# Turning ten of a kernel's sixteen feed-forward chunks by VectorE and a DRAM trip instead of by TensorE, on one core

## The reference

```
x = x + 0.5 * ffn(LN(x))      # FFN1
x = x + attention(LN(x))      # 16 heads of 8 features
x = x + 0.5 * ffn(LN(x))      # FFN2

ffn(x):  h = x @ W1' ; h = gelu(h + b1)          # 512 hidden features
         y = h @ W2' + b2
         W1' = W1.T + scale * (products of two normalized tokens of this batch)
         W2' the same for W2, from other tokens of the first 16
attention(x): q', k' = exp(q R/sqrt8 - |q|^2/16), the same for k
         kv = k'.T @ v  per batch and head;  out = q' @ kv / (sum q' + 1e-8) @ Wo.T + bo
```

## Time and profile before

| | before |
|---|---|
| median of three runs | 175.92 us (175.82 to 176.13) |
| time of the profiled execution | 174.35 us |
| its span (first to last instruction) | 172.6 us |
| TensorE busy | 166.8 us (97%), 1132 matmuls |
| VectorE busy | 127.4 us (74%) |
| ScalarE busy | 123.2 us (71%) |
| GpSimd busy | 69.4 us (40%) |
| bytes moved | 9.06 MB |

### The profile page before, as it was taken

How to read it: one execution, slowest core, us unless ns; L and a number is a source line. 1 busy time by engine, 2 the same in 40 slices (tenths; PEclk the granted TensorE clock), 3 DMA queues, 4 the chain that set the end, 5 groups by cost and what they waited for, 6 DMA issues and landing times.

```text
span 172.6 us, 3454 instructions
## 1 busy us (share of the span) xinstructions
PE 166.8 (97%) x1132; PEld 148.8 (86%) x1132; DVE 127.4 (74%) x446; ACT 123.2 (71%) x241; POOL 69.4 (40%) x85
## 2 busy tenths in 40 slices
PE   6999999999999999999999999899999999999993
PEld 6976998898899989768788898789899989898893
DVE  1888798977967647899999999998957664651111
ACT  3498669598796958779955499986894757557500
POOL 4522196232188089862522544004451399200000
PEclk9999999999999999999999999999999999999999
DMA  4993100404000000000000004310005003521203
GB/s 107 291 281 100 50 0 3 124 4 122 2 0 4 0 2 4 0 0 0 0 0 6 0 4 122 91 36 2 4 8 176 0 0 88 161 90 32 66 13 108
DMA packets 17009, 9.06 MB, mean 53 GB/s; under 512 B 1008, under 2 KB 16608, under 8 KB 16992
## 3 DMA queue, kind: packets, MB, share of 16 engines
q1 hardware_dynamic: 16704, 8.85, 17.4%
q10 hardware_dynamic: 288, 0.00, 0.1%
HBM read 6.69 MB, written 2.15 MB: 51 GB/s over the span
## 4 chain that ended last, share of the span: by engine, by line
PE 90%; DVE 5%; issue 2%; ACT 1%; POOL 0%; POOLq 0%; DVEq 0%; ACTq 0%
PE quad L728 32%; PE quad L712 9%; PE quad L713 9%; PE quad L714 9%; PE ps_t L677 4%; PE quad L745 4%; PE quad L663 4%; PE quad L747 3%; PE quad L746 3%; PE ps_g L763 3%; PE ps_m L700 2%; PE ps_t L785 2%; PE ps_r L752 1%; DVE s L604 1%; PE ps_g L728 1%
## 5 line engine op out<-in xcount | busy, mean ns | idle before, releaser
L728 PEld LDWEIGHTS quad<-w2e,gl 128*128 128x128 f32 x496 | 59.9, 192 | 2.4 <-ACT gl L432 0.2
L728 PE MATMUL quad<-w2e,gl 128*128 128x128 f32 x496 | 60.7, 275 | 0.0
L432 ACT ACTIVATE gl<-quad,cols 128x512 f32<-128x512 f32 x64 | 43.5, 686 | 20.6 <-PE quad L714 20.3
L712 PE MATMUL quad<-xh,w1h 128*128 128x512 f32 x64 | 28.7, 448 | 0.6 <-DVE w1l L568 0.2
L342 POOL TENSOR_TENSOR rstd<-veps,mhalf 128x4 f32<-128x4 f32 (+1 forms) x16 | 16.1, 1011 | 31.3 <-DVE veps L124 29.5
L399 ACT ACTIVATE xn<-X,nmr,rstd 128x128 f32<-128x128 f32 x61 | 24.8, 484 | 3.6 <-DVE nmr L499 3.6
L713 PE MATMUL quad<-xl,w1h 128*128 128x512 f32 x64 | 25.3, 395 | 0.0
L714 PE MATMUL quad<-xh,w1l 128*128 128x512 f32 x64 | 25.2, 394 | 0.0
L595 DVE TENSOR_TENSOR X<-quad,X 128x512 f32<-128x512 f32 (+1 forms) x16 | 10.8, 673 | 15.6 <-PE quad L728 9.9
L363 POOL TENSOR_TENSOR X<-X,b2h 128x512 f32<-128x512 f32 x16 | 20.6, 1311 | 4.1 <-issue 4.1
L374 POOL TENSOR_TENSOR qn<-qk,zr 128x512 f32<-128x512 f32 x8 | 8.6, 1081 | 23.7 <-DVE zr L625 23.6
(11 more groups left out here) (108 smaller groups left out, 279.7 us busy)
## 6 DMA issues: line engine op xcount, KB each, us to landing
ev<-token_rows SPq DMA_DIRECT2D x7, 512.0 KB, 3.7
X<-in_x_dram SPq DMA_DIRECT2D x7, 256.0 KB, 6.4
out_dram<-X SPq DMA_DIRECT2D x7, 256.0 KB, 2.9
w1t<-in_w1t_dram SPq DMA_DIRECT2D x1, 256.0 KB, 3.6
w2n<-in_w2t_dram SPq DMA_DIRECT2D x1, 256.0 KB, 4.7
wa<-in_wa_dram SPq DMA_DIRECT2D x1, 256.0 KB, 6.7
out_dram<-X SPq DMA_DIRECT2D x2, 128.0 KB, 1.8
X<-in_x_dram SPq DMA_DIRECT2D x1, 192.0 KB, 3.3
```

Of the source, the lines that this page charges most:

```text
L432: act.activation(gl[:, f % 2, j], ps_h[j % 2], ACT.Gelu, bias=cols[:, j:j + 1]).then_inc(s_gelu, 1)
L712: pe.matmul(ps_h[j % 2], w1h[:, w, blk], xh[:, f % XT], start=True, stop=False)
L728: ins = pe.matmul(y[:, n * P:(n + 1) * P], gl[:, f % 2, j, n * P:(n + 1) * P], w2e[:, f // PER_B % 2, j], start=(j == 0), stop=(j == HB - 1))
```

## The change

- Chunks 4 to 7 and 10 to 15 no longer use TensorE's transposes. The new VectorE stage **blocks** transposes the 32x32 blocks of xn into the tile tq (a ring of two). SyncE's **put** writes tq to DRAM (256 KB), and **land** reads it back in four transfers of 64 KB whose pattern puts the blocks in their places, into the tile land (a ring of three). ScalarE's and VectorE's halves of **turn** then read land in SBUF instead of ps_t in PSUM. Chunks 0 to 3, 8 and 9 go on as before.
- Attention's inputs are still turned by TensorE, but xah and xal become rings of six chunks.
- **z_eps** goes from VectorE to GpSimd; the second half of **mix** (the copy of mo) goes from VectorE to ScalarE; batch 0's rounding of W1' (**first_w1h**) goes from VectorE to ScalarE.
- The first loads are issued in another order: X of chunk 3 ahead of W2, X of chunk 4 ahead of the bias rows, and the attention weights last. W2 is scaled in place.
- All five lists of ORDER are rewritten; **constants** now comes ahead of batch 1's weights.

The core of the diff (the rewritten lists are cut down to a few of their places):

```diff
+PE_TURNS = (0, 1, 2, 3, 8, 9)
+BY_DRAM = [f for f in range(FC) if f not in PE_TURNS]
+SQ = 32
+LAND, TQ, AH = 3, 2, 6
...
 "sp":
+        "rows.1 rows.2 put.4 land.4 put.5 rows.3 put.6 land.5 land.6 put.7 land.7 rows.4 rows.5 put.10 land.10 put.11 "
...
 "act":
+        "norm.0 rest.0 first_w1h.0 first_w1h.1 turn.0 norm.1 first_w1h.2 norm.2 turn.1 up.0.0 first_w1h.3 up.0.1 "
+        "load.0 up.0.2 up.0.3 turn.2 up.1.0 up.1.1 norm.3 up.1.2 norm.4 up.1.3 w1h.1 norm.5 turn.3 up.2.0 up.2.1 "
...
 "dve":
+        "scale.0 stats.0 moments.0 rest.0 norm.0 stats.1 rest_norm.0 odd.0 moments.1 first_w1.0 first_w1.1 stats.2 "
+        "norm.1 moments.2 first_w1.2 first_w1.3 stats.3 norm.2 turn.0 first_w1l.0 first_w1l.1 moments.3 first_w1l.2 "
+        "stats.4 stats.5 first_w1l.3 turn.1 moments.4 w2.0 norm.3 norm.4 stats.6 stats.7 moments.5 moments.6 turn.2 "
+        "odd.1 norm.5 w1.1 constants.0 b2h.0 w1l.1 blocks.4 blocks.5 w2.1 norm.6 turn.3 down.0.3 moments.7 astats.0 "
...
 "pe":
+        "warm_up.0.0 warm_up.0.1 lead.0 select.0 turn.0 select.1 warm_up.0.2 turn.1 up.0.0 up.0.1 up.0.2 up.0.3 "
+        "turn.2 up.1.0 up.1.1 down.0.0 up.1.2 up.1.3 down.0.1 turn.3 down.0.2 down.0.3 down.1.0 down.1.1 up.2.0 "
...
+        def turned(f):
+            return as_tiles(ps_t[:]) if f in PE_TURNS else in_order(land[:, by_dram(f) % LAND])
...
+                if stage == "put":
+                    sp.wait_ge(s_tr, by_dram(i) + 1)
+                    sp.dma_start(folded[i], tq[:, by_dram(i) % TQ]).then_inc(s_put[i], 16)
+                if stage == "land":
+                    sp.wait_ge(s_put[i], 16)
...
+                    for b in range(D // SQ):
+                        place = slice(SQ * b, SQ * (b + 1))
+                        sp.dma_start(land[place, by_dram(i) % LAND].rearrange("p (q c) -> p q c", q=P // SQ),
+                                     folded[i].rearrange("(q p) (b c) -> b p q c", p=SQ, c=P)[b]).then_inc(s_land[i], 16)
...
                 if stage == "turn":
-                    act.wait_ge(s_xt, i + 1)
+                    if i in PE_TURNS:
+                        act.wait_ge(s_xt, by_pe(i + 1))
+                    else:
+                        act.wait_ge(s_land[i], 16 * D // SQ)
                     wait(act, s_u, HB * (i - XT + 1))
-                    act.activation(xh[:, i % XT], ps_t[:], ACT.Copy).then_inc(s_hi, 1)
+                    act.activation(as_tiles(xh[:, i % XT]), turned(i), ACT.Copy).then_inc(s_hi, 1)
...
+                if stage == "blocks":
+                    dve.wait_ge(s_xn, normed(i, NT - 1))
+                    k = by_dram(i)
+                    if k >= TQ:
+                        dve.wait_ge(s_put[BY_DRAM[k - TQ]], 16)
+                    dve.transpose(folding(tq[:, k % TQ]), as_tiles(flat(xn[:, i % XN]))).then_inc(s_tr, 1)
```

More of the change, by code:

```diff
@@ L34 @@
     "sp": (
-        "rows.1 rows.2 rows.3 rows.4 rows.5 rows.6 down.8.3 rows.7 down.9.3 down.10.3 down.11.3 down.12.3 down.13.3 "
-        "down.14.3 down.15.3 "
+        "rows.1 rows.2 put.4 land.4 put.5 rows.3 put.6 land.5 land.6 put.7 land.7 rows.4 rows.5 put.10 land.10 put.11 "
+        "rows.6 put.12 land.11 land.12 put.13 rows.7 put.14 land.13 land.14 down.8.3 put.15 land.15 down.9.3 "
+        "down.10.3 down.11.3 down.12.3 down.13.3 down.14.3 down.15.3 "
     ),
     "pool": (
[5 rows of a table removed]
[5 rows of a table added]
     ),
     "act": (
[13 rows of a table removed]
[13 rows of a table added]
     ),
     "dve": (
[17 rows of a table removed]
[18 rows of a table added]
     ),
     "pe": (
[17 rows of a table removed]
[17 rows of a table added]
     ),
@@ L150, in build @@
         xl = sb("xl", [P, XT, TOK], F32R)
+        tq = sb("tq", [P, TQ, TOK])
+        land = sb("land", [P, LAND, TOK])
         abst = sb("abst", [P, CHUNKS, NT, 6])
@@ L233, in build @@
             sem(n) for n in ("r_bst", "r_mv", "r_veps", "r_rstd", "r_nmr", "r_xn", "s_lead")]
+        s_tr = sem("s_tr")
+        s_put = [sem(f"s_put{f}") for f in range(FC)]
+        s_land = [sem(f"s_land{f}") for f in range(FC)]
         s_u, s_gelu, s_d = sem("s_u"), sem("s_gelu"), sem("s_d")
@@ L261, in xslot, with by_dram, by_pe, folding @@
             return f if f < CHUNKS else f + CHUNKS
+        def by_dram(f):
+            return len([k for k in BY_DRAM if k < f])
+        def by_pe(f):
+            return len([k for k in range(f) if k in PE_TURNS])
+        def folding(t):
+            return t.rearrange("p (b n i) -> p n b i", n=NT, i=SQ)
+        def in_order(t):
+            return t.rearrange("p (q n i) -> p n q i", n=NT, i=SQ)
+        def turned(f):
+            return as_tiles(ps_t[:]) if f in PE_TURNS else in_order(land[:, by_dram(f) % LAND])
+        def as_tiles(t):
+            return t.rearrange("p (n q i) -> p n q i", n=NT, i=SQ)
         def normed(f, n):
@@ L369, in _ @@
                                        rows[:, D:2 * D].unsqueeze(1).to_broadcast([P, NT, D]), ALU.add).then_inc(a_xb, 1)
+                if stage == "z eps":
+                    pool.wait_ge(s_zs, i + 1)
+                    wait(pool, s_zr, i)
+                    pool.tensor_scalar(zs[:, 1], zs[:, 0], Z_EPS, None, ALU.add).then_inc(s_ze, 1)
                 if stage == "z":
@@ L394, in _ @@
                     act.wait_ge(s_nmr, i + 1)
-                    wait(act, s_xt, i - XN + 1)
+                    if i - XN in PE_TURNS:
+                        act.wait_ge(s_xt, by_pe(i - XN + 1))
+                    elif i >= XN:
+                        act.wait_ge(s_tr, by_dram(i - XN + 1))
                     wait(act, s_rows, 16 * ((i - XN) // PER_B))
@@ L406, in _ @@
                 if stage == "turn":
[L408 removed]
+                    if i in PE_TURNS:
+                        act.wait_ge(s_xt, by_pe(i + 1))
+                    else:
+                        act.wait_ge(s_land[i], 16 * D // SQ)
                     wait(act, s_u, HB * (i - XT + 1))
[L410 removed]
+                    act.activation(as_tiles(xh[:, i % XT]), turned(i), ACT.Copy).then_inc(s_hi, 1)
                 if stage == "aturn":
                     act.wait_ge(a_xt, i + 1)
[L413 removed]
+                    wait(act, s_qk, NT * (i - AH + 1))
+                    act.activation(xah[:, i % AH], ps_m[:], ACT.Copy).then_inc(a_hi, 1)
+                if stage == "first w1h":
+                    act.wait_ge(s_w1r, i + 1)
+                    act.activation(w1h[:, 0, D * i:D * (i + 1)], w1r[:, i], ACT.Copy).then_inc(s_w1h, 1)
                 if stage == "w1h":
@@ L451, in _ @@
                     act.activation(qt[:, i % QT], ps_r[:], ACT.Copy).then_inc(s_qte, 1)
+                if stage == "mix":
+                    b = i[0]
+                    act.wait_ge(m_mp, b + 1)
+                    wait(act, s_o, PER_B * b)
+                    act.activation(mo[:], ps_m[:, D:2 * D], ACT.Copy).then_inc(m_mo, 1)
                 if stage == "gram" and i % PER_B == PER_B - 1:
@@ L534, in _ @@
                         dve.wait_ge(s_hi, PER_B * i + 1)
-                    dve.tensor_tensor(od[:, i], (lead if i == 0 else ps_t)[:, 2:2 + 4 * LORA:2], scl[:],
+                    dve.tensor_tensor(od[:, i], (lead if i == 0 else ps_t if PER_B * i in PE_TURNS else land[:, by_dram(PER_B * i) % LAND])[:, 2:2 + 4 * LORA:2], scl[:],
                                       ALU.mult).then_inc(s_od, 1)
@@ L549, in _ @@
-                    blocks = LORA if i == 0 else 1
-                    for k in range(blocks):
-                        mine = range(LORA * k // blocks, LORA * (k + 1) // blocks)
-                        part = slice(D * mine[0], D * (mine[-1] + 1))
-                        for j in mine:
-                            if i == 0:
-                                dve.wait_ge(k_sel, min(j + 1, 3))
-                            even = picked[j] if i == 0 else ev[:, i % 2, j]
-                            dve.scalar_tensor_tensor(out=w1r[:, j], in0=even, scalar=od[:, i, j:j + 1],
-                                                     in1=w1t[:, j * D:(j + 1) * D], op0=ALU.mult,
-                                                     op1=ALU.add).then_inc(s_w1r, 1)
-                        if i == 0:
-                            dve.wait_ge(s_w1r, mine[-1] + 1)
-                            dve.tensor_copy(w1h[:, 0, part], flat(w1r[:])[:, part]).then_inc(s_w1h, 1)
-                            dve.wait_ge(s_w1h, mine[-1] + 1)
-                            dve.tensor_tensor(w1l[:, 0, part], flat(w1r[:])[:, part],
-                                              w1h[:, 0, part].bitcast(F32), ALU.subtract).then_inc(s_w1, 1)
@@ new lines, in _ @@
+                    dve.wait_ge(s_ev, 16 * i)
+                    dve.wait_ge(s_w1, LORA * i)
+                    for j in range(LORA):
+                        dve.scalar_tensor_tensor(out=w1r[:, j], in0=ev[:, i % 2, j], scalar=od[:, i, j:j + 1],
+                                                 in1=w1t[:, j * D:(j + 1) * D], op0=ALU.mult,
```

(17 more changed lines are left out.)

46 lines of the change are left out of this document (19 added, 27 removed), and 97 rows, old and new, of the table ORDER.

## The result

| | before | after |
|---|---|---|
| median of eight runs each, taken in turns | 175.31 us (174.34 to 176.13) | 174.1 us (173.8 to 174.93) |
| ratio, with 95% interval | | 0.9933 [0.9906, 0.9959] |
| profiled execution, own time / span | 174.35 / 172.6 us | 174.93 / 173.2 us |
| the same, profiled a second time | | 173.42 / 171.7 us |
| matmuls | 1132 | 1092 |

The change is faster, by 1.2 us (0.67%, interval 0.4 to 0.9%). The forecast was 2.8 us. Two profiles of after differ by 1.5 us between themselves, as much as the thing to be explained, so their difference has to be understood first.

What follows compares the result with a forecast made beforehand. TensorE was taken to bound the kernel, with VectorE equally full in attention. Terms -4.4 + 1.2 + 0.3 = -2.9, put at -2.8 after small late things, took 175.92 to 173.1 us; range 170.9 to 175.8.

Steps and rivals of the forecast that it cites:

- TensorE's saving: On TensorE in FFN1 and FFN2: ten turns of four transposes removed, 0.44 us each, 4.4 us saved.
- The start: Before the first up: VectorE's longer list ahead of xl.0 makes up.0.0 start 1.2 us late, at about 12.7.
- Batch 1's weights: In FFN1, w1l.1 for up.2.0: VectorE and TensorE get there level, so 0, upper end 0.7 us.
- blocks and the trip: Ten chunks: blocks 0.7 us each on VectorE, 7.4 us from blocks to last landing, narrowest FFN1 margin 0.8 us.
- Attention: Attention stretch, VectorE decides: added and removed work give 0 to 0.5 us more, taken as 0.3.
- xl from SBUF: Ten subtractions on VectorE reading two SBUF tiles: 2 us more there, inside its idle time, counted as 0.
- late landings: ScalarE's queue standing behind a late land, TensorE after it: counted 0, upper end 2 us over all.
- The likeliest case: The forecast itself, whole kernel: 2.8 us faster, 173.1 us, own range 172.0 to 174.2; chance 0.53.
- rival B: VectorE eats most of the saving at start, w1l.1 and attention: 175.2 us; sign TensorE waiting over 1.5 us; chance 0.17.
- A: Whole saving kept: start costs 0.4 us or less, stalls between attention and FFN2 go, 171.3 us; chance 0.20.
- C: ScalarE waits for late landings; trips of 11 us or more use up the 2.9, 182 us at 14.6; chance 0.10.

Runs made afterwards that it cites:

- 2: Changed kernel with its ten trip chunks turned by TensorE again (no blocks, put, land), all else as after: 177.17 us, ratio 1.0101 to the kernel before.
- 3: Changed kernel with chunks 4 to 7 turned by TensorE again, only chunks 10 to 15 by the DRAM trip: 176.32 us, ratio 1.0071 to the kernel before.
- 5: Changed kernel with only GpSimd's list reordered, no instruction added or removed: 172.62 us, ratio 0.9886 to the kernel before.
- 7: Changed kernel with the copy of mo back on VectorE: 174.24 us, ratio 0.9961 to the kernel before.
- 8: Changed kernel with attention reordered and FFN2's preparation spread otherwise, in all five lists: 174.68 us, ratio 0.9981 to the kernel before.
- 4: Changed kernel with xl of the ten trip chunks formed from old ps_t content in PSUM instead of land: 173.32 us, ratio 0.9887 to the kernel before.

## Why the prediction was right or wrong

- **TensorE's saving, -4.4: right as content, 3.0 as time** once the trip's costs are taken off it (2). 1092 matmuls; the four turns of FFN1 are worth 1.8 us (3), against 1.75 forecast.
- **The start, +1.2: right.** +0.99 with the clock's step at about the same moment (6.0 and 6.2 us). Lead at 7.11 (forecast 7.3), first up at 12.49 (12.7).
- **Batch 1's weights, 0: right.** FFN1 is even 0.5 us shorter than forecast.
- **blocks and the trip: the durations right, the margins too wide.** blocks took 698 ns (0.7 forecast), the write 2.9 us (2.9), the read 2.2 (2.7). But the whole trip was forecast at 7.4 us for a SyncE queue that is otherwise idle; it took up to 12.5, as SyncE's other work stands in between (3). Chunks 12 and 14, forecast with 5 us of margin, had none: ScalarE waited 0.94 and 0.89 us for their landings, while chunk 4, called the narrowest of FFN1, was in time. The group of blocks:

```profile
L606 DVE STREAM_TRANSPOSE tq<-xn 128x512 f32<-128x512 f32 x10 | 6.8, 698 | 0.7 <-ACT xn L459 0.6
```

- **Attention, +0.3: this term failed. It was 2.1** (+0.76 in length, though 1.33 us of TensorE's work had moved ahead of it). By counting rows VectorE was to gain 0.3 us there. It is busy 0.8 us longer over the stage (45.77 against 44.96), of which two veps that stand beside GpSimd's long operations are 1.24: without them it would have 0.4 less than before, so the count was good. What was missed is that rows are not constants: VectorE's operations stand while GpSimd's long ones run, and the new lists let two of them meet there, where before none did. Reordering GpSimd alone gives 1.1 of the 1.8 back (5). The rest, about 0.7, stays open: pieces of it are a wait of TensorE of 0.82 us for ex at 73 us and one of 0.4 for ScalarE's copy of gs, which are in both profiles of after and in 5. It is not mo's home (7), the order in 8 doesn't make attention shorter than 5 does, and z_eps' home was not tried by itself.
- **xl from SBUF and late landings, each 0: 0.8 us in FFN2.** The price of xl was right (2 us on VectorE), its value wrong: 0.5 to 0.66 us comes back in FFN2 when xl reads PSUM (4), and a single xl cost the first profile 0.66 in FFN1. "Inside VectorE's idle time" was an average over 56 us; where the weights or the turned chunk are needed next, there is none. The landing of chunk 12 makes 0.4 (0.94 us of wait against 0.34).

The likeliest case was right in sign, and the result lies between it and rival B. That it came so near is in part luck: the start and FFN1 took 0.7 us less than forecast and hid a part of the 2.6 us that attention and FFN2 took more. The sign that was set for B, TensorE waiting over 1.5 us in attention for VectorE, was seen, just over that line (its two waits for ex alone, 1.8 us). B had it from a crowded VectorE list, together with a late start and late weights, neither of which came. A did not happen. C's sign, a wait of ScalarE for land, was set too low: waits of 0.9 us were there, and they take from the gain without turning it round. C's own terms also don't meet its threshold: at a trip of 11 us for all, 2 x 3 + 2 x 1 less 3 of cover is 5 us, which is more than the 2.9 that it was said to use up.

## What to carry to other kernels

Read the durations of an engine's rows as conditional on what its neighbour runs at the same time: before work goes to GpSimd, look which VectorE operations will start under its long ones, and move those, not the engine's total. Idle time summed over a stage covers nothing at the one place where its consumer waits. Price a chain of transfers by what stands between its links in the issuing engine's list, not by the links alone. After a change that takes work off the bounding engine, look for the order of the lists around it: here moving a handful of entries in one list was worth 0.8 us (intervals overlap), two thirds of the change itself.
